# Bias attention written out head by head, with the next head's q beside block 6, its row bias before its column bias, the turn one tile later, and turns and biases over 128 rows or columns

## What is computed

```python
q, k, v = split(x @ w_qkv)                      # 2 images of 64x64 positions, 4 heads of 32
rw = rel_logits_1d(pos_q, pos_emb_w)            # column bias: query x position along the row
rh = rel_logits_1d(pos_q.T12, pos_emb_h)        # row bias
scores = einsum('bnqd,bnkd->bnqk', q, k) * scale + rw + rh
attn = softmax(scores, axis=-1)
out = einsum('bnqk,bnkd->bnqd', attn, v)        # 4096 queries x 4096 keys for each head and image
```

## Time and profile before

| | us |
|---|---|
| runs: 9182.60, 9195.72, 9189.42; median | 9189.42 |
| the profiled execution, its own time | 9187.98 |
| its span, first to last instruction | 9185.4 |
| mean granted TensorE clock, share of full speed | 0.939 |
| PE busy over the span (matmul) | 8246.9 |
| PE line 659 idle before it for the DVE maxima, 57 times | 43.7 |
| PE line 676 idle for the DMA of the low row bias, 8 times | 31.2 |
| PE line 636 idle with nothing to wait for ("issue"), 6 times | 24.9 |
| PE line 612 idle for DVE's column-bias split, 8 times | 22.7 |

### The profile page before, as it was taken

How to read it: one execution, slowest core, us unless ns; L and a number is a source line. 1 busy time by engine, 2 the same in 40 slices (tenths; PEclk the granted TensorE clock), 3 DMA queues, 4 the chain that set the end, 5 groups by cost and what they waited for, 6 DMA issues and landing times. The chain is left out here.

```text
span 9185.4 us, 139845 instructions
## 1 busy us (share of the span) xinstructions
PE 8246.9 (90%) x42040; PEld 6695.8 (73%) x42040; DVE 7029.1 (77%) x7887; ACT 5755.2 (63%) x14820; POOL 6726.0 (73%) x3596
## 2 busy tenths in 40 slices
PE   6999999999999767899999999967999989888798
PEld 4766767667676533788888888855786868888775
DVE  6776767767677666899999999976777746999734
ACT  4877878778787634777777777732565633445304
POOL 3876868678696725899999999950686825999605
PEclk9999999999999977899999999988999999988898
DMA  2111111111111245544444444453000010000000
GB/s 93 28 40 30 41 40 31 39 30 41 27 41 33 65 163 207 144 106 105 109 104 107 106 106 108 107 189 142 29 26 18 23 50 19 1 1 1 20 8 19
DMA packets 480129, 596.14 MB, mean 65 GB/s; under 512 B 273736, under 2 KB 294480, under 8 KB 471568
## 3 DMA queue, kind: packets, MB, share of 16 engines
q1 hardware_dynamic: 479504, 588.17, 22.4%
HBM read 349.14 MB, written 157.03 MB: 55 GB/s over the span
## 5 line engine op out<-in xcount | busy, mean ns | idle before, releaser
L817 POOL TENSOR_TENSOR l_probs_low<-l_probs,l_probs_high 128x512 fp32r<-128x512 f32 x1792 | 2384.9, 1359 | 787.2 <-ACT l_probs_high L787 770.4
L1542 POOL TENSOR_TENSOR m_c_h<-m_h,m_c 128x2048 f32<-128x2048 f32 x520 | 2341.8, 4561 | 51.1 <-DVE m_h L1529 50.9
L1529 DVE TENSOR_TENSOR_SCAN m_h<-m_decay,m_ps_x 128x1024 f32<-128x1024 f32 x1040 | 2273.2, 2263 | 95.8 <-issue 67.8
L1442 PE MATMUL m_ps_y<-m_c_h,m_ident 128*128 128x256 f32 x8320 | 1981.7, 381 | 2.1 <-POOL m_c_h L1542 2.1
L873 DVE TENSOR_REDUCE l_max_by_row<-l_ps_all 128x8 f32<-128x512 f32 x2048 | 1358.5, 686 | 522.7 <-PE l_ps_all L636 444.1
L1442 PEld LDWEIGHTS m_ps_y<-m_c_h,m_ident 128*128 128x128 f32 x8320 | 1513.5, 191 | 173.2 <-POOL m_c_h L1542 4.0
L785 ACT ACTIVATE l_probs<-l_ps_all 128x512 f32<-128x512 f32 x2048 | 1238.8, 605 | 454.8 <-PE l_ps_all L677 310.9
L787 ACT ACTIVATE l_probs_high<-l_ps_all 128x512 fp32r<-128x512 f32 x2048 | 1234.3, 603 | 0.0
L2095 POOL TENSOR_TENSOR l_probs_low<-l_probs,l_probs_high 128x512 fp32r<-128x512 f32 x512 | 660.4, 1296 | 584.1 <-ACT l_probs_high L2078 567.6
L2548 POOL TENSOR_TENSOR s_late<-s_late,s_products 128x1024 f32<-128x1024 f32 x352 | 858.0, 2477 | 307.0 <-ACT s_products L2530 306.9
L1466 ACT ACTIVATE m_b_diagonals<-m_steps,m_b_rows 128x32 fp32r<-128x32 f32 x4160 | 966.7, 306 | 3.0 <-DMA m_b_rows<-b_t 3.0
(11 more groups left out here) (382 smaller groups left out, 13819.1 us busy)
## 6 DMA issues: line engine op xcount, KB each, us to landing
m_delta_u<-du_t SPq DMA_DIRECT2D x1040, 128.0 KB, 3.8
m_c<-c_windows SPq DMA_DIRECT2D x130, 512.0 KB, 4.3
l_q_and_row_bias<-l_q_parts SPq DMA_DIRECT2D x64, 512.0 KB, 5.0
du_t<-m_delta_u_high SPq DMA_DIRECT2D x128, 256.0 KB, 3.0
du_t<-m_delta_u_low SPq DMA_DIRECT2D x128, 256.0 KB, 3.0
ys<-m_y SPq DMA_DIRECT2D x256, 126.0 KB, 5.0
m_direction<-ys SPq DMA_DIRECT2D x12, 2048.0 KB, 13.7
l_xn<-xn SPq DMA_DIRECT2D x8, 2048.0 KB, 8.0
```

The lines of the kernel that those rows point to most:

```text
L817: pool.tensor_tensor(pl[:, slot, :], pt[:, slot, :], f(ph[:, slot, :]), ALU.subtract).then_inc(low_pool, 1)
L1442: ins = pe.matmul(y_ps[:, group % 2, 0:DIRS * SPAN].rearrange("p (d t) -> p d t", d=DIRS), ident[:, :], ch[:, group % CH, :, n, :], start= ...
L1529: dve.tensor_tensor_scan(h[:, u % H, :], decay[:, pair % 2, ct, k % 2, :, :].rearrange("p n t -> p (n t)"), x_ps[:, u % X, :], 0.0, ALU.mu ...
L1542: pool.tensor_tensor(ch[:, group % CH, 2 * pair % DIRS:2 * pair % DIRS + 2, :, :].rearrange("p d n t -> p d (n t)"), h[:, 2 * pair % H:2 * ...
```

## The change

- PE's loop over heads is gone: all 8 heads are written out. ACT keeps its loop over heads but writes the blocks out; POOL now loops over heads, with 8 blocks written out.
- `plan`: the q jobs of the next head go to tiles 23 to 30 of block 6 (tile number minus 32), one a tile; h at tiles 1 to 4 of block 7, two a tile; w at 5 to 12, one a tile; k 7 and 6 first, all k by tile 22. `FIRST_UNITS` now covers tiles 15 to 26. Two banks' worth of k (1024 keys instead of 512) is put aside for block 7 (`ASIDE`).
- `turn_bias` for the next head's block 0 at tile 26 (28), its `turn` at tile 29 of block 7 (in the seam before). In the other blocks the turn goes from tile 19 to 20.
- `start` issues six units of block 1 (`FILL`) between v and the scores; block 0 has 26 of them left.
- Row bias: the high part has its own semaphore and its four DMAs are issued before the low ones; for block 0 the four low ones are issued by ACT, behind its last exponential of the head. The common part of `ql` has its own semaphores. `copy_q` waits for block 6's scores.
- Line 620 now uses 128-column tables (the second 64 columns give rows that nobody reads), `turn_bias` transposes 128 rows (the lower 64 zeroed once by POOL) and `turn` spreads the maxima over 128 columns.

```diff
-    EARLY, READY = 12, 19
-    LAST = slice(L - TW, L)
+    EARLY, READY, FILL = 12, 19, 6
+    ASIDE = 2 * TW
+    LAST = slice(L - ASIDE, L)
+    TURN_FIRST = 29
-    plan = [(0, "q", 0), (0, "q", 1), (1, "q", 2), (2, "q", 3), (2, "q", 4), (3, "q", 5), (4, "q", 6), (4, "q", 7),
...
+    plan = [(t - 9, "q", t) for t in range(NTB)]
+    plan += [(1, "h", 0), (1, "h", 1), (2, "h", 2), (2, "h", 3), (3, "h", 4), (3, "h", 5), (4, "h", 6), (4, "h", 7), (5, "w", 0), (5, "k", 7),
...
-    FIRST_UNITS = {16: 3, 17: 3, 18: 3, 19: 3, 20: 3, 21: 3, 22: 2, 23: 2, 24: 2, 25: 2, 26: 2, 27: 2, 28: 2}
+    FIRST_UNITS = {15: 2, 16: 2, 17: 3, 18: 3, 19: 3, 20: 3, 21: 3, 22: 3, 23: 3, 24: 3, 25: 2, 26: 2}
...
             def copy_rows(it, j):
                 row, slot = it * NTB + j, j % 2
-                sp.wait_ge(shifted, row + 2)
-                for g in range(GROUPS):
-                    for first, part in ((D, rh), (D + NEAR, rl)):
+                for first, part in ((D, rh), (D + NEAR, rl)):
+                    if part is rh:
+                        sp.wait_ge(high_made, row + 1)
+                    elif j:
+                        sp.wait_ge(shifted, row + 2)
+                    else:
+                        break
+                    for g in range(GROUPS):
                         sp.dma_start(f(ql[first:first + NEAR, slot, g, :]), f(part[g * NEAR:(g + 1) * NEAR, :])).then_inc(ql_in[slot], 16)
...
-                        ins = pe.matmul(o[0:SIDE, k * SIDE:(k + 1) * SIDE], table[:, SIDE - 1 - x:2 * SIDE - 1 - x], moving, start=True, stop=True)
+                        ins = pe.matmul(o[:, k * SIDE:(k + 1) * SIDE], table[:, SIDE - 1 - x:3 * SIDE - 1 - x], moving, start=True, stop=True)
...
-                    ins = pe.matmul(ps[:, TURNED, k * SIDE:(k + 1) * SIDE], r32[:, at], ident[0:SIDE, 0:SIDE], start=True, stop=True)
+                    ins = pe.matmul(ps[:, TURNED, k * SIDE:(k + 1) * SIDE], bias_rows[:, at], ident[:, 0:SIDE], start=True, stop=True)
...
-                    ins = pe.matmul(ps[0:SIDE, TURNED, k * P:(k + 1) * P], mx[:, k:k + 1].to_broadcast((P, SIDE)), ident[:, :], start=True, stop=True)
+                    ins = pe.matmul(ps[:, TURNED, k * P:(k + 1) * P], mx[:, k:k + 1].to_broadcast((P, P)), ident[:, :], start=True, stop=True)
...
-                        if i == READY:
+                        if i == READY + 1:
                             turn(row + 1)
...
-                    if following:
+                    if following == 1:
+                        begin(it, 1, i - KT)
+                    if following == 2:
                         begin(it, 1, i)
...
             def start(it, off):
                 row = it * NTB + off * NTB
-                turn(row)
                 for t in range(KT // 2, KT):
                     project_v(it, off, t)
-                made(it, off, number["k", 6] + 1)
...
+                made(it, off, number["k", 5] + 1)
+                for u in range(FILL):
+                    max_unit(row + 1, 1, u)
+                for i in range(2):
+                    score(it + off, 0, i)
...
-            with pe.Fori(0, ITS - 1) as it:
+            for it in range(ITS):
                 for j in range(NTB):
-                    attend(it, j, j == NTB - 1)
-            for j in range(NTB):
-                attend(ITS - 1, j, False)
+                    attend(it, j, max(0, j + 3 - NTB) if it + 1 < ITS else 0)
...
-                        work += [(READY + 0.1, take_maxima, row + 1), (READY + 0.3, shift, row + 1)]
+                        work += [(READY + 0.1, take_maxima, row + 1), (READY + 1.3, shift, row + 1)]
```

112 lines of the change are left out of this document (69 added, 43 removed).

## The result

The changed kernel takes **9204.3 us** in the median against 9189.5 for the kernel before: ratio 1.0017, 95% interval 1.0011 to 1.0023. It is 15 us slower where 93 less were forecast, and outside the range. Its profiled execution has a span of 9195.4 us, 10 more than before; the first attention alone is 13.8 longer (last exponential at 3181.1 instead of 3167.3), so the rest of the program moved by less than 4.

What follows compares the result with a forecast made beforehand. PE was taken to bound the kernel, with POOL next in a steady block. Terms -31, -22, -18, -9, 0, +11 and -23 summed to -92, from 9187.98 to 9096 us; the range was 9045 to 9150.

Steps and rivals of the forecast that it cites:

- Loop written out: Block 0 of heads 1 to 6: without the loop's jump, 5.1 us less six times, -31; bounds 24 and 31.
- Six units leave block 0: Block 0 of all eight heads: six fewer units save 2.8 us each, -22; bounds 1.4 and 3.8 a block.
- Bias transposes: Blocks 0 to 6: 128-row transposes avoid a shape change on PE, 0.33 us each, 56 times, -18.
- Turn one tile later: Turn at tile 20: no gain in blocks 0 to 5, 1.1 us in block 6 of eight heads, -9.
- q beside block 6: Eight q jobs add 6.9 us to block 6 and take the same 6.9 from block 7, sum 0.
- Rest of block 7: Block 7, seven times: 8.7 us added, 7.1 of waits and other time removed, +1.6 each, +11.
- The seam: Between heads, seven times: row-bias DMA wait goes, six units come in, 3.3 us less each, -23.
- The first head's start: Before the first exponential: gains about as much as its padded h and w matmuls cost, 0.
- D: Rival, chance 0.07: PE's straight code is fetched late, 4.03 us stalls, one a block giving 9322 us.
- B: Rival, chance 0.13: turn's 1.1 us also gained in 48 other blocks (9043), or padded h and w free (9059).

Runs made afterwards that it cites:

- b_straight: The kernel before with only TensorE's loop over heads written out: 9162.4 us, ratio 0.9972 to the kernel before.
- a_fill0: The changed kernel with no units of block 1 in the seam, all 32 in block 0 again: 9217.2 us, ratio 1.0033 to the kernel before.
- b_turn20: The kernel before with only the turn, and DVE's shift with it, one tile later at tile 20 in blocks 0 to 6: 9179.0 us, ratio 0.9996.
- a_turn19_narrow: The changed kernel with the turn back at tile 19, row-bias transposes over 64 rows and the turn with 64 columns: 9149.9 us, a single run.
- a_turn64: The changed kernel with only the turn back at 64 columns: 9119.6 us, ratio 0.9932 to the kernel before.
- a_hw64: The changed kernel with h and w matmuls back at 64 columns of weights: 9180.7 us, ratio 0.999 to the kernel before.
- a_low_first: The changed kernel with DVE taking tile 29's low half ahead of the shift in block 7: 9177.5 us, ratio 0.9997 to the kernel before.

## Why the prediction was wrong, step by step

1. **Loop written out, -31.** Right in kind, near the lower bound in size: 27 (b_straight).
2. **Six units leave block 0, -22.** Mis-sized: 4.8 us a block, 38.5 (a_fill0). I had bounded it by 3.8. In a_fill0's block 0 of head 2, PE waits over 0.2 us for DVE's reductions at five places, 2.4 us in sum, where the changed kernel has two with 1.4; and the clock is lower, which the bound left out. With the loop's 27, the transposes' 3, the 9 of the cut and 3 that b_turn20 shows for the late turn, these are 80 of block 0's 82.7.
3. **Bias transposes, -18.** Right: 0.32 to 0.34 a time (a_turn19_narrow). Two parts of it cancel: the transposes take 0.81 until the next matmul, not 0.90, and that one 0.31, not 0.23.
4. **Turn one tile later, 0 in blocks 0 to 5 and -9 in block 6.** This is the step that failed. For the late turn alone the zero in steady blocks holds (b_turn20). The fault is in "the shift as well": it was to start later, and I took it as if it kept its length. The earlier trace rows show it from 636.27 to 638.80, 2.53 us for three operations. These are the other two, and POOL beside them:

```profile
636.99 1.17 DVE L888 CAST l_row_bias_high<-l_row_bias_shifted 64x512 fp32r<-64x512 f32 x1
638.19 0.68 DVE L889 TENSOR_TENSOR l_row_bias_low<-l_row_bias_shifted,l_row_bias_high 64x512 fp32r<-64x512 f32 x1
```

```profile
629.39 8.49 POOL L817 TENSOR_TENSOR l_probs_low<-l_probs,l_probs_high 128x512 fp32r<-128x512 f32 x6
639.33 2.99 POOL L817 TENSOR_TENSOR l_probs_low<-l_probs,l_probs_high 128x512 fp32r<-128x512 f32 x2 [1.46 <-ACT l_probs_high L787]
```

The cast is 1.17 long there and 0.42 elsewhere, and ends 0.28 us behind POOL's operation (637.88); I never looked at POOL. Its next operation came 1.14 us behind the start of the last one, since PE's wait for the maxima holds the exponentials back. The turn at tile 20 takes that wait away and leaves a margin of 0.28 (b_turn20). The turn at 128 columns takes away 0.3 more: from the unit ahead of it to the second matmul behind it, 1.36 us instead of 1.68. So POOL's operation comes 0.06 us ahead of the shift's last. Then 1.07 us of DVE become 1.1 us of PE in a block, and 2.7 where the clock falls as well: +56.7 instead of -13. Narrowing the turn alone (a_turn64) takes back all of that 70. The prediction counted the 0.2 of the wide turn as a gain that is waited off later; it was the trigger of the loss. I also named the third unit as the place of the wait; it is the second. The -9 of block 6 failed too: its two parts, 0.76 and 0.2, make 0.96 and not 1.1, b_turn20 shows 0.85 a block, and block 7 takes it back.
5. **q beside block 6, 0.** By the terms a block 6 should take 38.0 + 6.9 - 1.1 - 0.3 = 43.5; it takes 45.0 or 45.1. The 38.0 is 1.28 short by the cut, which leaves 0.2 or 0.3. A tile with a q job takes 1.79 us between exponentials where one without takes 0.95: a job costs 0.84, as forecast. With the turn back at tile 19 block 6 is 45.3, with the narrow turn of a_turn64 44.6; how that divides stays open, since in four heads the first q job waits 0.4 for the long shift and the three heads without that wait take 45.0 as well.
6. **Rest of block 7, +11.** The sum is right (-41.4 against -37 with q's part), by two errors that cancel. h and w at 128 columns have the paces forecast (h 1.70 against 0.90, w 0.81 against 0.59), but a_hw64 gives back only 3.2 of the 5.3: the rest lay beside other waits, so the waits that I let go were worth 2 less.
7. **The seam, -23.** Failed, at the sentence that the shift "ends ahead of the last weighing". The weighing of tile 29 needs a low half that DVE takes, and it is queued behind the shift, which lasts 3.05 us there (1303.14 to 1306.19): 2.34 of wait, shown by a_low_first. The six units cost 4.03, not 3.3. Together 3.0 a seam, and in two seams the v matmuls ran at the low clock: 6.7 us instead of 3.5. The DMA cover went as forecast. The sum itself is a little too high: 514.67 - 512.1 and 0.6 make 3.2 and not 3.3.
8. **The first head's start, 0.** Failed: +22.9. I set the padded h and w against the other gains at full clock; there an h matmul takes 0.205. a_hw64 takes 15.7 of it back, the six units are 2.8 (a_fill0), and some 4 stay open.

No rival named what happened. D had the sign but its mechanism is refuted: no "issue" stall appeared at the units, and b_straight gains. B's remark that the shift may be shorter in other blocks has the right place and the wrong sign. The range was made of errors in the size of PE's terms; none of them let another engine's operation change its length.
